# A stationary operand of 128 columns in place of 4 for the product that turns the row maxima

## The reference, cut to what matters

```python
qkv = x @ qkv_w + qkv_b
...
q, k = _rope(q, k, S, D)
scale = math.sqrt(D)
attn = jnp.einsum('bhqd,bhkd->bhqk', q, k) / scale
attn = jax.nn.softmax(attn, axis=-1)
out = jnp.einsum('bhqk,bhkd->bhqd', attn, v)
```

## Time and profile before

| what | value |
|---|---|
| three timed runs | 1840.63, 1849.58, 1852.35 us |
| median | 1849.58 us |
| profiled execution, first to last instruction | 1847.4 us |
| profiled execution, time of its own | none given; the span stands for it |
| TensorE busy, products | 1740.1 us, 94% |
| VectorE, ScalarE, GpSimd busy | 1444.6, 1407.5, 1430.4 us |
| granted TensorE clock, mean | 0.977 of full speed |

### The profile page before, as it was taken

One profiled execution on the slowest core, in us unless ns is written; L12 is line 12 of the kernel. 1 busy time (PEld: TensorE's weight loads), 2 busy tenths in 40 slices (PEclk: granted clock), 3 DMA queues, 4 the chain that ended last, 5 costly groups with the idle time before them and its releaser, 6 DMA issues. The chain is left out here.

```text
span 1847.4 us, 53971 instructions
## 1 busy us (share of the span) xinstructions
PE 1740.1 (94%) x22856; PEld 1101.7 (60%) x22856; DVE 1444.6 (78%) x2658; ACT 1407.5 (76%) x1737; POOL 1430.4 (77%) x851
## 2 busy tenths in 40 slices
PE   5999999999999999999999999986899999978997
PEld 2466666666666666666666666675556666653454
DVE  5888888888888888888888887535988888845785
ACT  2688888888888888888888888943998888853463
POOL 6699999999999999999999999974765566624122
PEclk9899999999999999999999999998999999989998
DMA  5101010111101010101010010050111111110000
GB/s 142 25 20 31 19 31 23 27 26 28 26 24 30 21 31 19 31 23 28 23 31 23 24 26 4 2 165 18 41 40 36 37 37 37 34 26 1 1 0 24
DMA packets 71080, 56.89 MB, mean 31 GB/s; under 512 B 29196, under 2 KB 64184, under 8 KB 70840
## 3 DMA queue, kind: packets, MB, share of 16 engines
q1 hardware_dynamic: 70840, 53.44, 11.5%
HBM read 14.54 MB, written 1.05 MB: 8 GB/s over the span
## 5 line engine op out<-in xcount | busy, mean ns | idle before, releaser
L278 POOL TENSOR_TENSOR ah_probs_lo<-ah_probs,ah_probs_hi 128x1024 f16<-128x1024 f32 x512 | 1072.8, 2132 | 78.8 <-ACT ah_probs L487 78.7
L542 DVE TENSOR_REDUCE ah_part_max<-ah_p_m 128x1 f32<-128x512 f32 x1024 | 669.2, 685 | 120.9 <-PE ah_p_m L342 111.1
L484 ACT ACTIVATE ah_probs_hi<-ah_p_s 128x1024 f16<-128x1024 f32 x512 | 531.2, 1038 | 190.0 <-PE ah_p_s L358 178.8
L487 ACT ACTIVATE ah_probs<-ah_p_s 128x1024 f32<-128x1024 f32 x512 | 532.4, 1040 | 0.0
L372 PE MATMUL ah_p_o<-ah_v_hi,ah_probs_hi 128*128 128x65 f16 x4096 | 470.5, 195 | 5.7 <-POOL ah_probs_lo L278 5.1
L374 PE MATMUL ah_p_o<-ah_v_lo,ah_probs_hi 128*128 128x64 f16 x4096 | 470.5, 193 | 0.0
L376 PE MATMUL ah_p_o<-ah_v_hi,ah_probs_lo 128*128 128x65 f16 x4096 | 470.3, 194 | 0.0
L372 PEld LDWEIGHTS ah_p_o<-ah_v_hi,ah_probs_hi 128*128 128x128 f16 x4096 | 383.0, 98 | 84.3 <-DVE a_attn L565 12.3
L374 PEld LDWEIGHTS ah_p_o<-ah_v_lo,ah_probs_hi 128*128 128x128 f16 x4096 | 378.4, 98 | 91.3
L342 PE MATMUL ah_p_m<-ah_k_hi_lo,ah_q_hi_twice 128*128 128x512 f16 x1024 | 393.9, 385 | 6.6 <-DMA ah_max_q_lo<-ah_lo 3.1
L357 PE MATMUL ah_p_s<-ah_q_hi_twice,ah_k_hi_lo 128*128 128x512 f16 x1024 | 388.6, 379 | 0.8 <-ACT ah_probs L487 0.4
(11 more groups left out here) (316 smaller groups left out, 3090.0 us busy)
## 6 DMA issues: line engine op xcount, KB each, us to landing
ba_v_skew<-ba_v_own SPq DMA_DIRECT2D x64, 129.0 KB, 2.3
ah_q_hi_twice<-ah_hi SPq DMA_DIRECT2D x128, 64.0 KB, 2.0
ah_k_hi_lo<-ah_hi SPq DMA_DIRECT2D x64, 64.0 KB, 1.9
ah_one_k_hi<-ah_hi SPq DMA_DIRECT2D x64, 64.0 KB, 2.0
ah_k_hi_lo<-ah_lo SPq DMA_DIRECT2D x64, 64.0 KB, 2.0
ah_max_q_lo<-ah_lo SPq DMA_DIRECT2D x64, 64.0 KB, 2.0
ah_w_head<-in_w_heads SPq DMA_DIRECT2D x16, 160.0 KB, 2.4
bw_rot<-in_rot SPq DMA_DIRECT2D x4, 512.0 KB, 10.3
```

The lines of the kernel that those rows point to most:

```text
L278: pool.tensor_tensor(pl[:, p % RW, :, :], pb[:, p % RP, :, :], ph[:, p % RW, :, :], ALU.subtract).then_inc(lo_pool, 1)
L484: act.activation(ph[:, p % RW, :, :], p_s[:, p % 2, :, :], ACT.Exp, scale=HD ** -0.5)
L487: act.activation(pb[:, p % RP, :, :], p_s[:, p % 2, :, :], ACT.Exp, scale=HD ** -0.5).then_inc(exp_done, 1)
L542: dve.tensor_reduce(part[:, t, 2 * half + b:2 * half + b + 1], p_m[:, b, :], AX, ALU.max).then_inc(maxed, 1)
```

## The change

`neg_max` becomes 128 columns wide. Columns 4 to 127 are set to zero once, on VectorE in the start-up, and the first wait for constants on TensorE wants this memset as well. `negate_max` writes columns 0 to 3 as before. The product of line 347 takes the whole tile as its stationary operand and so writes 128 rows of `p_a`; rows 4 to 127 are zero and have no reader. It streams the same 128 columns of the identity.

```diff
@@ -156,7 +156,7 @@
         part = sc.sb("part_max", [P, TPC, 4])
-        negm = sc.sb("neg_max", [P, TPC], F16)
+        negm = sc.sb("neg_max", [P, P], F16)
         identh = sc.sb("ident_f16", [P, P], F16)
...
@@ -290,7 +290,7 @@
                     mm.then_inc(x_turned, 1)
-                pe.wait_ge(consts, 1)
+                pe.wait_ge(consts, 2)
...
@@ -344,7 +344,7 @@
                 def turn_max(e):
                     pe.wait_ge(m_done, e + 1)
-                    pe.matmul(p_a[0:TPC, 0:P], negm[:, :], identh[:, :], start=True, stop=True).then_inc(m_turned, 1)
+                    pe.matmul(p_a[:, 0:P], negm[:, :], identh[:, :], start=True, stop=True).then_inc(m_turned, 1)
...
@@ -546,7 +546,7 @@
-                    dve.tensor_reduce(negm[:, :], part[:, :, :], AX, ALU.max, negate=True).then_inc(m_done, 1)
+                    dve.tensor_reduce(negm[:, 0:TPC], part[:, :, :], AX, ALU.max, negate=True).then_inc(m_done, 1)
...
@@ -567,6 +567,7 @@
                 dve.tensor_copy(identh[:, :], ident[:, :]).then_inc(consts, 1)
+                dve.memset(negm[:, TPC:P], 0.0).then_inc(consts, 1)
```

## The result

The changed kernel takes 1837.53 us, the median of 15 runs (1827.55 to 1842.9), against 1848.92 us for the kernel before in 15 runs (1840.63 to 1852.39). The ratio is 0.994 with a 95% interval of 0.9928 to 0.9953: 0.6% faster. The profiled execution spans 1836.3 us against 1847.4, 11.1 us less, where 10.9 had been forecast; for the median 1838.7 had been forecast.

The account below looks back on a forecast made before the run. TensorE was taken to bound the heads. 57 x 0.19 + 0.1 = 10.9 us saved takes the span from 1847.4 to 1836.5; with the median 2.2 us over the span, 1838.7 us, range 1830 to 1846.

Parts of the forecast that it names:

- The price of line 347: In each turn of the heads, line 347 costs TensorE 0.09 us extra going in and 0.094 going out; 0.19 saved.
- the pairs in the local layers: Start distances around lines 1128, 1134 and a 128*128 to 128*64 change, read as 0.09 to 0.10 us per change of form.
- every change of the stationary operand's form costs: On TensorE, any change of operand form takes about 0.09 us, and line 347 has two.
- The pair read for the way back: From 128*64 back to 128*128: 0.13 us after a 65-column product against 0.03, read as 0.10 us.
- The wider load: Line 347's operand load takes 98 ns instead of 80, beside line 342's product of 0.215 us, so costs 0.
- The rival in which it stands in the open: Line 347's full load is not hidden: 0.12 us instead of 0.09 going in, 1.7 us slower, 1851.3 us; 4%.
- one change stays: Line 347's way out is slow for another reason, so only 0.09 x 57 = 5.1 us go: 1844.4 us; 6%.
- the form is not the cause: The wait before line 347 costs the time, not its operand's form, so nothing changes: 1849.6 us; 6%.
- the two cases at 1849.6 and above: Line 347 gains nothing (1849.6 us, 6%), or its wider load is unhidden (1851.3 us, 4%); the prediction wrote 12%.
- the moved tiles: probs, probs_hi and probs_lo, behind neg_max, move by 224 bytes and slow GpSimd's steps: slower by over 1%; 2%.
- Its need of 18.00 us in a turn with a split: GpSimd needs 16.76 us for eight steps plus 1.24 every fourth turn, 18.00 against TensorE's 18.01; under 0.3 us lost.
- The last stretch: From 1102.96 us to the heads' end, GpSimd runs 54 steps without pause; TensorE's savings there give 0.1 us.

## Why the prediction was right

**The bound.** TensorE leads the heads: confirmed by the turn, which fell from 18.20 to 18.00 us on average over the 57 turns when TensorE lost 0.20 us of work, and rose to 18.25 and 18.45 when it gained some.

**The price of line 347.** The forecast was 0.09 in and 0.094 out, with up to 0.01 behind, taken as 0.19. Measured: 0.20, since all three terms came in full.

**The cause.** It was put on the form of the operand, from the pairs in the local layers. That the form is behind it was shown by the run that restores 4 columns with all else kept. The sentence "every change of the stationary operand's form costs" was too wide: 128*65 and 128*96 stand between 128*128 operands at no cost. The three pairs that I had read all had 64 columns or fewer on one side, so they could not tell the two readings apart. The change itself goes to 128, where both give the same. The pair read for the way back also had a float32 product behind it, line 1157 in the earlier trace rows, so its 0.10 us was not of the change alone; that the way out costs 0.094 is shown by the turn here and not by that pair.

**The wider load** was priced at 0 beside line 342's product: the load takes 98 ns and the way in is 0.22. The rival in which it stands in the open would have 0.33 there. That rival had one thing right that the prediction's own sum did not use: the 80 ns load of the narrow operand did stand in the open, as it began with its product. Making it wide let it run ahead. What keeps a load back at a change of the cut was not separated from the change itself; the way in is 0.309 us with a load of 80 ns and with one of 106, so it is not the length of the load that sets it. The rivals "one change stays" and "the form is not the cause" fall by the 0.05 on the way out and by the run with 4 columns restored. The 12% that the prediction gives to "the two cases at 1849.6 and above" are 10% for two; with the moved tiles they are 12.

**GpSimd.** Its need of 18.00 us in a turn with a split was the closest call of the sum. Those turns take 18.00 like the others, its idle time behind a split is gone, and the run with less TensorE work shows it as the limit there. The last stretch gives nothing back, as the run with the wide form in it alone shows.

**The sum.** Forecast were 57 x 0.19 + 0.1 = 10.9 us. From the run of line 347 at 69 us to the one at turn 58 it is 57 x 0.20 = 11.4. From there to the end of the heads it is 0.1 less (109.1 us before, 108.9 after), as taken. The run at 69.4 us of the earlier trace rows stands one turn before 86.7 now, at 68.7, so 0.7 us come from in front of it. This is scatter and not a gain: in the five other runs with 64 columns or fewer it lies at 68.5 to 70.2, in the five others with 65 or more at 68.3 to 69.7. Together 12.2 us, and the span fell by 11.1: the local layers took 1.2 us more (the last 0.1 is rounding), from the first to the last run of line 1128 (1129 and 1130 in later kernels). Their rows (range of starts) before, after, and in the run with the wide form in the last stretch alone:

```profile
L1128 PE MATMUL ba_p_s<-bw_ident_f,ba_negmax x256: 219/219/230, 1292.7 to 1630.5; 128*128 128x128 f16 x128
```

```profile
L1129 PE MATMUL ba_p_s<-bw_ident_f,ba_negmax x256: 218/219/231, 1280.5 to 1619.5; 128*128 128x128 f16 x128
```

```profile
L1130 PE MATMUL ba_p_s<-bw_ident_f,ba_negmax x256: 218/219/230, 1293.8 to 1628.8; 128*128 128x128 f16 x128
```

That is 337.8, 339.0 and 335.0 us for the same work in the same order. The stretch varies by 4 us from execution to execution, and so the agreement of 10.9 with 11.1 within 0.2 us is better than the method, and in part luck: a price per turn that came out 0.5 us larger over the 57 turns and 0.7 us of scatter in the start-up met 1.2 us of scatter in the local layers. What varies there was not tried.

## What to carry to other kernels

Read what a small product costs from the starts of its neighbours, not from its duration: 128 columns cost 0.056 us in a stream of like products and 0.25 with their two changes of the array's cut. A stationary operand of 64 columns or fewer among wider ones is worth padding with zeros to 65 or more, where TensorE leads and the product in front is long enough to cover the load; two narrow ones cost less next to each other (18.25 us a turn against 18.45), and the narrow ones that ran side by side were worth keeping. Before counting a saving in each turn, work out what the next engine needs in its fullest turn: here it was 18.00 us against 18.01, and the next 0.23 us lost a quarter.

## What the runs showed that was not expected

The price has a sharp edge between 64 and 65 columns. An operand of 64 columns is dearer than one of 4: the way out takes 0.176 us by the start times (0.18 in the rows) against 0.150, and the product's record is 243 ns long instead of 218. Its load takes 106 ns instead of 80 and stands in the open, so the 26 ns on the way out are as long as what the load takes more; no run separates the two. With 65 columns the load takes 112 ns and costs nothing, since it begins ahead of its product, beside line 342's. Four 64*64 products of 512 columns, each of them 0.40 us in the record, together last 0.41 us, while two whole ones last 0.59. The page "TensorEngine Tiling (Array Packing)" of the Trainium skill states under Key Properties that tiles run independently, and the trace agrees.
